# A macaron block of eight batches on one core: first step reordered, last batch's end by tiles, output product in three fp32r passes

## The chip, the core and the metric

The kernel runs on one core of a Trainium2 chip. The core has five engines that work side by side, each through its own list of instructions in order: TensorE (matmuls), VectorE, ScalarE, GpSimd and SyncE, which here issues most of the transfers. They wait for each other through semaphores. TensorE, VectorE, ScalarE and GpSimd read SBUF, TensorE writes PSUM. The metric is the device time of one execution in microseconds; lower is better.

## What is computed

The input x has 8 batches of 512 tokens with 256 channels, all float32. In short:

```
x  = x + 0.5 * adapter(norm(x))             adapter: 8 selected 256x256 matrices, weighted and summed, one bias
h  = layernorm1(norm(x));  hh = h one token earlier
k, v, r = three 256x256 products of (h*tm + hh*(1-tm)), tm its own for each
y  = wkv(k, v): a running, decaying weighted mean over the tokens, made of max and exp
a  = norm(x) + (sigmoid(r) * y) Wo           the output product
h2 = layernorm2(a), shifted and mixed in the same way
kk = relu(h2k Wck)^2  (1024 channels);   kv = kk Wcv;   c = a + sigmoid(h2r Wcr) * kv
x  = x + c
x  = x + 0.5 * adapter(norm(x))
```

## The kernel before

**Stages and steps.** One batch is one unit. Its work is in two halves: the front (first adapter, norm, time mix, k, v, r, wkv, output product, second norm) and the channel part (keys, gate, values, last sum, second adapter). A loop runs over e from 0 to 7. Step e does the channel part of batch e beside the front of batch f = e + 1, and the second adapter of batch e - 1. Ahead of the loop stands the setup, with the adapters' weights and the front of batch 0; behind it the end of the last batch. No planner sets the order: each engine's list is written out by hand, and each semaphore counts up over the whole run.

**TensorE in a step:** `turn_x1(f)` (transposes to channels), keys 0 to 3, `turn_x2(e-1)`, k and v, keys 4 and 5, r, keys 6 and 7, `second_product(e-1)`, the gate product, half of the values of token tile 0, `output_product(f)`, the rest of tile 0 and tile 1, `turn_xa(f)`, tiles 2 and 3. The first adapter, k, v, r, the output product and the values run as float32 (one matmul is two records in the trace). Keys, gate and second adapter run in three fp32r passes instead: each operand is split in a high part (ScalarE's copy to fp32r) and a rest (VectorE's subtraction), and high x high, high x rest and rest x high are summed. The output product is float32: `to_tokens` (L300) with `rwkv` and `wo_sb`, 8 matmuls of 256 columns.

**VectorE in a step:** `value_sum` and `value_stats` of the second half of batch e-1, `mixes(f)` (L848: xr, xk, xv), `gate_input_rest(e)` (L977), `second_rest(e-1)` (L952), `wkv_exponents(f)` (L864: per half a scan over k in PSUM and a subtraction to q), `wkv_states` (L872: a scan and a product per half), denominator, sums, numerator, quotient, `wkv_gated` (L907, ends in `rwkv`, L917), `add_second(e-1)` (L1011), `add_first(f+1)` (L809), `add_output(f)` (L919), `stats_x1`, `norm_output(f)` (L930), the first half of `value_sum(e)`, `norm_first(f+1)`, `mix_ck`, `key_input_rest` (L966), `mix_cr`.

**GpSimd in a step:** the bias for half 1 of batch e-1, a root, `mix_r(f)` (L1161), `hold_exponents(f)` (L1167: clamps of q; L1171 on the second half alone, and `state_exponentials` on ScalarE waits for it), one half of `bias_to_x(f+1)` (L1149) when the sums `aa` are done and the other when `rwkv` is done, `attention_sum(f)` (L1174), roots, and `bias_to_x2(e, 0)` (L1181).

**ScalarE in a step:** `h1_of`, relu and square of the eight key blocks with the high parts and `scaled_difference(f)` (L661, which `mix_r` waits for) between, the exponentials, the reciprocal, the tanh of r and of the gate (`channel_gate`, L626), `residual_of`, statistics of x of batch f+2 from batch `ON_ACT` on (`stats_x`, L530), `h2_of` and what follows it.

**Places.** q, the states and the exponentials share the tile `work`. `xr`, `rwkv`, `xcr` and `xcr_lo` are tiles of 128 x 1024 float32 values. Of the last batch the last sum, transposes and second adapter are done in two halves of two token tiles each.

## Time and profile before

| | us |
|---|---|
| median of 3 runs | 445.81 (445.05 to 447.63) |
| the profiled execution, its whole time | 445.64 |
| its span in the trace | 443.9 |
| busy: TensorE | 426.9 (96%) |
| busy: VectorE | 379.4 (85%) |
| busy: ScalarE | 296.0 (67%) |
| busy: GpSimd | 180.0 (41%) |

The table is from one profiled execution. The span is the time from the first to the last event in the trace; the whole time has a little more around it. An engine is busy while one of its instructions runs. Two records of one engine that follow closely overlap by some 0.08 us, so durations of neighbours sum to slightly more than their distance. Matmul records overlap more: the distance between starts is what one costs. A timeline joins equal instructions in a row: x4 says how many, and the duration is that of all.

### The profile page before, as it was taken

The numbers are of one execution on the slowest core, as the hardware profiler recorded it, in microseconds if no ns is written. First come the engines' busy times: TensorE is split into PE (matmuls) and PEld (weight loads), VectorE is DVE, ScalarE is ACT, GpSimd is POOL, SyncE is SP. The second block draws the span as 40 slices with busy tenths as digits, with TensorE's granted clock in tenths as the row PEclk, the third lists the DMA queues.
The fourth block names the chain that finished last, engine by engine and source line by source line (L and its number), as shares of the span: only waits on it lengthen the run. The fifth ranks groups of instructions, "written<-read, shape, count | busy, mean of one in ns | idle before, by whom it ended". The sixth has DMA issues, their size and how long they took to land. (4 is left out here: it accounts for less than half of the span.)

```text
span 443.9 us, 6124 instructions
## 1 busy us (share of the span) xinstructions
PE 426.9 (96%) x2014; PEld 332.6 (75%) x2014; DVE 379.4 (85%) x769; ACT 296.0 (67%) x541; POOL 180.0 (41%) x161
## 2 busy tenths in 40 slices
PE   8989996989999999999999999999999999999995
PEld 8865873568857885698759885888579865988984
DVE  3989989799999899989999999989998999776134
ACT  1158767695789568984888578956894489736400
POOL 1545053626561465427352746156533444042010
PEclk9999998999999999999999999999999999999999
DMA  6990001001000200011001100010001000100101
GB/s 206 390 396 29 1 0 47 1 1 49 1 0 1 83 13 0 0 50 47 1 0 47 49 1 1 0 48 1 0 1 49 2 0 0 49 0 1 48 1 48
DMA packets 15954, 18.51 MB, mean 42 GB/s; under 512 B 1066, under 2 KB 13618, under 8 KB 15922
## 3 DMA queue, kind: packets, MB, share of 16 engines
q1 hardware_dynamic: 14522, 17.05, 10.8%
q10 hardware_dynamic: 1400, 1.07, 0.8%
q8 instruction: 16, 0.26, 0.2%
q14 instruction: 16, 0.13, 0.1%
HBM read 13.92 MB, written 4.19 MB: 41 GB/s over the span
## 5 line engine op out<-in xcount | busy, mean ns | idle before, releaser
L423 PE MATMUL pair<-wcv_sb,kk 128*128 128x256 f32 x512 | 114.3, 379 | 0.0
L423 PEld LDWEIGHTS pair<-wcv_sb,kk 128*128 128x128 f32 x512 | 96.1, 190 | 12.4
L393 PE MATMUL pair<-xck_hi,wck_hi 128*128 128x512 f32 x128 | 58.0, 453 | 0.7 <-ACT kk L620 0.7
L394 PE MATMUL pair<-xck_hi,wck_lo 128*128 128x512 f32 x128 | 50.6, 395 | 0.0
L397 PE MATMUL pair<-xck_lo,wck_hi 128*128 128x512 f32 x128 | 50.6, 395 | 0.0
L1139 POOL TENSOR_TENSOR x2b<-xs,bias_bc 128x512 f32<-128x512 f32 x15 | 25.6, 1706 | 58.1 <-DVE xs L993 58.1
L1139 POOL TENSOR_TENSOR x<-x,bias_bc 128x512 f32<-128x512 f32 x14 | 18.1, 1298 | 63.4 <-DVE rwkv L917 36.3
L620 ACT ACTIVATE kk<-pair 128x512 f32<-128x512 f32 x64 | 36.4, 594 | 8.1 <-PE pair L397 8.1
L564 ACT ACTIVATE h<-pair,vec 128x512 f32<-128x512 f32 x16 | 11.6, 774 | 42.7 <-PE pair L297 42.7
L624 ACT ACTIVATE kk<-kk 128x512 f32<-128x512 f32 x64 | 37.8, 639 | 0.5
L1119 POOL TENSOR_TENSOR rstd_x<-vare_x,nhalf 128x4 f32<-128x4 f32 (+1 forms) x25 | 30.3, 1213 | 17.5 <-DVE vare_x L777 16.2
L1179 POOL TENSOR_TENSOR xs<-x,xa 128x512 f32<-128x512 f32 x16 | 20.5, 1283 | 39.8 <-DVE xa L923 39.6
L1165 POOL TENSOR_TENSOR xr<-xr,h 128x512 f32<-128x512 f32 x16 | 19.4, 1231 | 35.4 <-ACT xr L666 35.4
L393 PEld LDWEIGHTS pair<-xck_hi,wck_hi 128*128 128x128 f32 x128 | 24.1, 188 | 12.0 <-ACT kk L620 4.1
L325 PE MATMUL pair<-xk,wk_sb 128*128 128x512 f32 x64 | 30.6, 623 | 2.4 <-DVE xk L862 2.4
L394 PEld LDWEIGHTS pair<-xck_hi,wck_lo 128*128 128x128 f32 x128 | 24.1, 188 | 7.7 <-issue 3.3
L306 PE MATMUL pair<-wo_sb,rwkv 128*128 128x256 f32 x128 | 29.0, 380 | 0.4 <-issue 0.4
L325 PE MATMUL pair<-xv,wv_sb 128*128 128x512 f32 x64 | 28.8, 592 | 0.0
L325 PE MATMUL pair<-xr,wr_sb 128*128 128x512 f32 x64 | 28.8, 592 | 0.0
L397 PEld LDWEIGHTS pair<-xck_lo,wck_hi 128*128 128x128 f32 x128 | 24.0, 187 | 6.3 <-DVE xck_lo L971 0.4
L306 PEld LDWEIGHTS pair<-wo_sb,rwkv 128*128 128x128 f32 x128 | 24.2, 190 | 4.0 <-issue 0.7
L875 DVE TENSOR_TENSOR_SCAN work<-work 128x512 f32<-128x512 f32 x16 | 19.6, 1226 | 8.0 <-ACT work L679 8.0
(144 smaller groups left out, 1008.6 us busy)
## 6 DMA issues: line engine op xcount, KB each, us to landing
x<-in_x_dram SPq DMA_DIRECT2D x8, 512.0 KB, 3.5
out_dram<-xs SPq DMA_DIRECT2D x16, 256.0 KB, 2.1
xt<-in_xt_dram SPq DMA_DIRECT2D x4, 512.0 KB, 7.8
work<-in_ffn_w_dram ACTq DMA_DIRECT2D x4, 256.0 KB, 4.5
work<-in_ffn_w_dram SPq DMA_DIRECT2D x4, 256.0 KB, 5.0
kk<-in_wck_dram SPq DMA_DIRECT2D x1, 1024.0 KB, 9.8
xs<-in_xt_dram SPq DMA_DIRECT2D x2, 512.0 KB, 10.9
wcv_sb<-in_wcv_dram SPq DMA_DIRECT2D x1, 1024.0 KB, 12.6
```

What stands on the lines that cost most here:

```text
L306: last = nc.tensor.matmul(bank_of(stage, b, i)[:, t * C:(t + 1) * C], src[:, h, tok:tok + P], w[:, h, :], start=h == 0, stop=h == CH - 1)
L325: last = nc.tensor.matmul(bank, w[:, h, o * P:(o + 1) * P], src[:, h, :], start=h == 0, stop=h == CH - 1)
L393: nc.tensor.matmul(key_bank(n), wck_hi[:, h, cols], xck_hi[:, h, :], start=h == 0, stop=False)
L394: nc.tensor.matmul(key_bank(n), wck_lo[:, h, cols], xck_hi[:, h, :], start=False, stop=False)
L397: last = nc.tensor.matmul(key_bank(n), wck_hi[:, h, cols], xck_lo[:, h, :], start=False, stop=h == CH - 1)
L423: last = nc.tensor.matmul(bank_of("kv", e, i)[:, t % TB * C:(t % TB + 1) * C], kk[:, n, tok:tok + P], wcv_sb[:, n, :], start=n == 0, stop= ...
L620: nc.scalar.activation(kk[:, n, :], key_bank(n), ACT.Relu).then_inc(relu_done, 1)
L624: nc.scalar.activation(kk[:, n, :], kk[:, n, :], ACT.Square).then_inc(sq_done, 1)
L875: nc.vector.tensor_tensor_scan(bb[:, h, 1:PAD], eb_s[:, h, 0:T], eb_v[:, h, 0:T], 0.0, ALU.mult, ALU.add).then_inc(bb_done, 1)
L1119: nc.gpsimd.tensor_tensor(dst, src, power, ALU.pow).then_inc(done, 1)
L1139: nc.gpsimd.tensor_tensor(dst, tile, bias_bc[:, :].rearrange("p (a c) -> p a c", a=1).broadcast_to([P, tiles, C]), ALU.add).then_inc(done, 1)
L1179: nc.gpsimd.tensor_tensor(tok_bank(xs[f % 2], i), tok_bank(x1[f % X1], i), tok_bank(xa, i), ALU.add).then_inc(xs_done, 1)
```

## The change

The output product of batches 1 to 7 is done in three fp32r passes, as the gate product is. Wo gets a high part and a rest once, `rwkv` for each batch: ScalarE copies (`output_input_high`, between the gate's two tanh), VectorE subtracts (`output_input_rest`, between the halves of `add_second`). The high part of `rwkv` lies in the tile of `xr`, its rest in its own tile, and `xcr_lo` now in the tile of `xcr`; `mixes` waits for the output product before it, `past_cr` for the gate product. In every step `gate_input_rest(e)` moves behind `wkv_exponents(f)`, `bias_to_x2(e, 0)` moves into the next step behind the wait for `aa`, and both halves of `bias_to_x` stand behind the wait for `rwkv`. In the first step the statistics of x of batch 2 move from VectorE to ScalarE, the attention sums of batch 0 ahead of the root for `norm_output(0)`, `h1_of(1)` ahead of a square, the high part of the gate's input behind relu 3, and two subtractions of weights behind the mixes and the exponents. The last batch's end goes in three parts: tiles 0 and 1, tile 2, tile 3, each with its own sum, transposes, copy, subtraction, product, addition and store.

```diff
-    ON_ACT = 3
+    ON_ACT = 2
     LAST = B - 1
+    LAST_PARTS = ((0, 1), (2,), (3,))
...
+        def in_place_of(other, name, shape):
+            return nc.alloc_sbuf_tensor_at(name, shape, F32R, offset=place[other])
...
+        wo_hi, wo_lo = sb("wo_hi", [P, CH, C], F32R), in_place_of("wo_sb", "wo_lo", [P, CH, C])
...
-        xcr_lo = sb("xcr_lo", [P, CH, T], F32R)
+        xcr_lo = in_place_of("xcr", "xcr_lo", [P, CH, T])
...
+        rwkv_hi, rwkv_lo = in_place_of("xr", "rwkv_hi", [P, CH, T]), in_place_of("rwkv", "rwkv_lo", [P, CH, T])
...
+            def three_passes(dst, t, own_hi, own_lo, w_hi, w_lo):
+                tok = slice(t * P, (t + 1) * P)
+                passes = [(own_hi[:, h, tok], w[:, h, :]) for h in range(CH) for w in (w_hi, w_lo)]
+                passes += [(own_lo[:, h, tok], w_hi[:, h, :]) for h in range(CH)]
+                for j, (own, other) in enumerate(passes):
+                    last = nc.tensor.matmul(dst, own, other, start=j == 0, stop=j == len(passes) - 1)
+                return last
...
+        LAST_KV = ((3, 0), (3, 1), (0, 0))
+        LAST_Y2 = ((1, 0), (1, 1), (0, 1))
...
+            for j in range(len(LAST_PARTS)):
+                sp.wait_ge(x3_done, 2 * LAST + j + 1)
+                sp.dma_start(some_tiles(tok_dram(out, LAST), j), some_tiles(xs[LAST % 2], j)).then_inc(stored[LAST % 2], 16)
...
             def output_product(f):
                 if f == 0:
                     pe.wait_ge(s_wo, 1)
-                pe.wait_ge(rwkv_done, 2 * f + 2)
-                to_tokens("o", rwkv, wo_sb, xa2_done, f, o_ps)
+                    pe.wait_ge(rwkv_done, 2 * f + 2)
+                    to_tokens("o", rwkv, wo_sb, xa2_done, f, o_ps)
+                    return
+                if f == 1:
+                    pe.wait_ge(s_wo_lo, 1)
+                pe.wait_ge(rwkv_lo_done, 2 * (f - 1) + 2)
+                for i in range(BANKS):
+                    take(pair_of("o", f), i, xa2_done, 2 * f + i + 1)
+                    for t in range(TB):
+                        last = three_passes(bank_of("o", f, i)[:, t * C:(t + 1) * C], i * TB + t, rwkv_hi, rwkv_lo, wo_hi, wo_lo)
+                    last.then_inc(o_ps, 1)
...
-            second_product_part(LAST, 0)
-            turn_x2_part(LAST, 1)
-            second_product_part(LAST, 1)
+            last_values(0, 0, range(HB))
+            last_values(0, 1, range(HB))
+            last_values(1, 2, range(HB // 2))
+            last_turn(0)
+            last_values(1, 2, range(HB // 2, HB))
+            last_values(2, 3, range(HB // 2))
+            last_second(0)
+            last_turn(1)
+            last_values(2, 3, range(HB // 2, HB))
+            last_second(1)
+            last_turn(2)
+            last_second(2)
...
+            def setup_wo_high():
+                nc.scalar.activation(wo_hi[:, :, :], wo_sb[:, :, :], ACT.Copy).then_inc(s_wo_hi, 1)
+            def output_input_high(f):
+                act.wait_ge(r_ps, 2 * f + 2)
+                for h in range(CH):
+                    act.wait_ge(rwkv_done, 2 * f + h + 1)
+                    nc.scalar.activation(rwkv_hi[:, h, :], rwkv[:, h, :], ACT.Copy).then_inc(rwkv_hi_done, 1)
...
             def past_cr(f):
-                past_of("cm_r", f, xcr, (xcr_lo_done, 2 * f))
+                past_of("cm_r", f, xcr, (cr_ps, 2 * f))
...
                 for i in range(BANKS):
+                    if i == BANKS - 1 and has(e + 1):
+                        output_input_high(e + 1)
                     act.wait_ge(cr_ps, 2 * e + i + 1)
                     nc.scalar.activation(tok_bank(thc, i), bank3(bank_of("cr", e, i)), ACT.Tanh, scale=0.5).then_inc(thc_done, 1)
...
             keep_first(5)
+            act.wait_ge(s_wo, 1)
+            setup_wo_high()
+            stats_x(2)
             keep_first(6)
...
                 if has(f) and e > 0:
                     h1_of(f)
                 key_relu(e, 0)
-                gate_input_high(e)
+                if e > 0:
+                    gate_input_high(e)
                 key_square(e, 0)
                 key_relu(e, 1)
-                key_square(e, 1)
                 if e == 0:
                     h1_of(f)
+                key_square(e, 1)
                 key_relu(e, 2)
                 key_square(e, 2)
                 key_relu(e, 3)
                 if e == 0:
+                    gate_input_high(e)
                     keep_first(7)
...
                     if f > 0 and c == 0:
                         dve.wait_ge(r_ps, 2 * f)
+                        dve.wait_ge(o_ps, 2 * f)
                     nc.vector.tensor_tensor(xr[:, c, :], h1[:, c, 1:PAD], h1[:, c, 0:T], ALU.subtract).then_inc(d1_done, 1)
...
+            def output_weight_rest():
+                dve.wait_ge(s_wo_hi, 1)
+                dve.wait_ge(o_ps, CH)
+                nc.vector.tensor_tensor(wo_lo[:, :, :], wo_sb[:, :, :], wo_hi[:, :, :].bitcast(F32), ALU.subtract).then_inc(s_wo_lo, 1)
+            def output_input_rest(f):
+                for h in range(CH):
+                    dve.wait_ge(rwkv_hi_done, 2 * (f - 1) + h + 1)
+                    nc.vector.tensor_tensor(rwkv_lo[:, h, :], rwkv[:, h, :], rwkv_hi[:, h, :].bitcast(F32), ALU.subtract).then_inc(rwkv_lo_done, 1)
...
             def gate_input_rest(f):
                 for h in range(CH):
                     dve.wait_ge(xcr_hi_done, 2 * f + h + 1)
-                    if f > 0 and h == 0:
-                        dve.wait_ge(cr_ps, 2 * f)
                     nc.vector.tensor_tensor(xcr_lo[:, h, :], xcr[:, h, :], xcr_hi[:, h, :].bitcast(F32), ALU.subtract).then_inc(xcr_lo_done, 1)
...
+            def last_sum(j):
+                dve.wait_ge(kv_ps, 2 * LAST + j + 1)
+                dve.wait_ge(thc_done, 2 * LAST + min(j, BANKS - 1) + 1)
+                nc.vector.scalar_tensor_tensor(some_tiles(thc, j), some_tiles(thc, j), 1.0, by_tiles(last_bank(LAST_KV, j), j), ALU.add, ALU.mult).then_inc(kvs_done, 1)
+                dve.wait_ge(kvs_done, 2 * LAST + j + 1)
+                dve.wait_ge(xs_done, BANKS * (LAST + 1))
...
             add_output(0)
+            output_weight_rest()
             norm_output(0)
             stats_x1(1)
             mix_ck(0)
             key_input_rest(0)
             norm_first(1)
             mix_cr(0)
-            second_weight_rest()
-            stats_x(2)
-            gate_weight_rest()
             for e in range(B):
                 f = e + 1
                 if has(e - 1):
@@ -1061,11 +1176,16 @@
                     value_stats(e - 1, 1)
                 if has(f):
                     mixes(f)
+                if has(e - 1) and has(f):
+                    second_rest(e - 1)
+                if e == 0:
+                    second_weight_rest()
+                if has(f):
+                    wkv_exponents(f)
+                if e == 0:
+                    gate_weight_rest()
                 gate_input_rest(e)
                 if has(f):
-                    if has(e - 1):
-                        second_rest(e - 1)
-                    wkv_exponents(f)
                     wkv_states(f)
                     wkv_denominator(f)
                     wkv_sums(f)
@@ -1076,6 +1196,9 @@
                     second_rest(e - 1)
                 if has(e - 1):
                     add_second(e - 1, 0)
+                if has(f):
+                    output_input_rest(f)
+                if has(e - 1):
                     add_second(e - 1, 1)
                 if has(f + 1):
                     add_first(f + 1)
@@ -1085,6 +1208,8 @@
                     stats_x1(f + 1)
                 if has(f):
                     norm_output(f)
+                if e == LAST:
+                    break
                 value_sum(e, 0)
                 value_stats(e, 0)
                 if has(f + 1):
@@ -1093,13 +1218,19 @@
                     mix_ck(f)
...
+            last_sum(0)
+            last_stats(0)
+            last_rest(0)
+            last_sum(1)
+            last_stats(1)
+            last_add(0)
+            last_rest(1)
+            last_sum(2)
+            last_stats(2)
+            last_rest(2)
+            last_add(1)
+            last_bias(2)
+            last_add(2)
...
             pool.wait_ge(s_decay, 2)
             mix_r(0)
             hold_exponents(0)
+            attention_sum(0, 0)
+            attention_sum(0, 1)
             inverse_std("xa", 0)
             first_inverses(1)
-            pool.wait_ge(xck_lo_done, CH)
-            attention_sum(0, 0)
-            attention_sum(0, 1)
             inverse_x(2)
             for e in range(B):
                 f = e + 1
@@ -1209,11 +1338,14 @@
                 if has(f):
                     mix_r(f)
                     hold_exponents(f)
+                if has(e - 1):
+                    if has(f):
+                        pool.wait_ge(aa_done, 2 * f + 2)
+                    bias_to_x2(e - 1, 0)
                 if has(f + 1):
-                    pool.wait_ge(aa_done, 2 * f + 2)
+                    pool.wait_ge(rwkv_done, 2 * f + 2)
                     bias_to_x(f + 1, 0)
-                    pool.wait_ge(rwkv_done, 2 * f + 2)
                     bias_to_x(f + 1, 1)
                 if has(f):
                     attention_sum(f, 0)
@@ -1223,10 +1355,13 @@
                     first_inverses(f + 1)
                 if has(f + 2):
                     inverse_x(f + 2)
-                bias_to_x2(e, 0)
-            for i in range(BANKS):
-                some = slice(i * TB, (i + 1) * TB)
-                pool.wait_ge(vare_done["x2"], LAST + i + 1)
+            for j in range(len(LAST_PARTS)):
+                if j < BANKS:
+                    pool.wait_ge(x2_done, 2 * LAST + j + 1)
+                    pool.wait_ge(x3_done, 2 * (LAST - 1) + 2)
+                    add_bias(some_tiles(x2b, j), some_tiles(xs[LAST % 2], j), len(LAST_PARTS[j]), x2b_parts[j])
+                some = slice(LAST_PARTS[j][0], LAST_PARTS[j][-1] + 1)
+                pool.wait_ge(vare_done["x2"], LAST + j + 1)
                 inverse_root(rstd["x2"][:, some], vare["x2"][:, some], nhalf[:, some], rstd_done["x2"])
```

## Rows read from the trace of the kernel before

**Rows 1.** Busy time by stretch: length, then PE, PEld, DVE, ACT, POOL, granted clock, DMA.

```profile
298.90:346.62 47.72, 47.57 (x226) 36.82 (x226) 44.94 (x91) 32.97 (x55) 22.95 (x20) 1.00 0.04 12
```

**Rows 2.** Chain that ended last (start, us, engine and line).

```profile
347.12 0.88 PE pair L297 x6
...
378.41 2.88 PE pair L319 x24
...
385.85 3.45 PE pair L306 x16
```

**Rows 3.** Timeline of TensorE: the transposes of two steps (start, duration; idle before in brackets).

```profile
346.62 1.38 PE L297 MATMUL pair<-ident,normed 128*128 128x128 f32 x8
...
394.32 1.04 PE L297 MATMUL pair<-ident,normed 128*128 128x128 f32 x8
```

**Rows 4.** Timeline of VectorE and TensorE, one step (start, duration; idle before in brackets).

```profile
316.60 1.21 DVE L867 TENSOR_TENSOR_SCAN work<-decay,pair 128x512 f32<-128x512 f32 x1
...
319.70 0.69 DVE L870 TENSOR_TENSOR work<-work,pair 128x512 f32<-128x512 f32 x1
321.12 1.23 DVE L875 TENSOR_TENSOR_SCAN work<-work 128x512 f32<-128x512 f32 x1 [0.73 <-ACT work L679]
...
323.20 1.23 DVE L875 TENSOR_TENSOR_SCAN work<-work 128x512 f32<-128x512 f32 x1 [0.28 <-ACT work L679]
...
334.53 1.28 DVE L917 TENSOR_TENSOR rwkv<-work 128x512 f32<-128x512 f32 x2
335.73 1.65 DVE L1016 SCALAR_TENSOR_TENSOR xs<-pair,rstd_x,x2b 128x256 f32<-128x256 f32 x4
337.30 1.66 DVE L824 SCALAR_TENSOR_TENSOR x<-xt,rstd_x,x 128x256 f32<-128x256 f32 x4
339.98 0.69 DVE L923 TENSOR_TENSOR xa<-xa,pair 128x512 f32<-128x512 f32 x1 [1.02 <-PE pair L306]
...
341.64 0.69 DVE L923 TENSOR_TENSOR xa<-xa,pair 128x512 f32<-128x512 f32 x1 [0.18 <-PE pair L306]
...
362.36 3.60 PE L325 MATMUL pair<-xk,wk_sb 128*128 128x512 f32 x8
362.92 1.28 DVE L955 TENSOR_TENSOR x2t_lo<-pair,x2t_hi 128x512 fp32r<-128x512 f32 x2
...
364.27 1.22 DVE L867 TENSOR_TENSOR_SCAN work<-decay,pair 128x512 f32<-128x512 f32 x1
```

**Rows 5.** Timeline of GpSimd and ScalarE in the same step.

```profile
320.49 2.01 POOL L1171 TENSOR_SCALAR work<-work,decay 128x512 f32<-128x512 f32 x1 [0.28 <-DVE work L870]
...
335.89 1.29 POOL L1139 TENSOR_TENSOR x<-x,bias_bc 128x512 f32<-128x512 f32 x1 [6.05 <-DVE rwkv L917]
...
335.10 0.60 ACT L631 ACTIVATE thc<-pair 128x512 f32<-128x512 f32 x1 [0.37 <-PE pair L411]
```

**Rows 6.** Timeline where VectorE and GpSimd meet; durations of L1165 (min/median/max).

```profile
76.50 1.29 DVE L982 TENSOR_TENSOR xcr_lo<-xcr,xcr_hi 128x512 fp32r<-128x512 f32 x2
76.82 3.15 POOL L1165 TENSOR_TENSOR xr<-xr,h 128x512 f32<-128x512 f32 x2 [3.27 <-ACT xr L666]
...
L1165 POOL TENSOR_TENSOR xr<-xr,h x16: 1085/1183/2097, 31.8 to 365.2; 128x512 f32<-128x512 f32 x16
...
159.45 2.55 POOL L1139 TENSOR_TENSOR x2b<-xs,bias_bc 128x512 f32<-128x512 f32 x1
...
160.91 2.24 DVE L971 TENSOR_TENSOR xck_lo<-xk,xck_hi 128x512 fp32r<-128x512 f32 x2
```

**Rows 7.** Timeline of the first step.

```profile
75.32 5.36 PE L325 MATMUL pair<-xk,wk_sb 128*128 128x512 f32 x8 [2.39 <-DVE xk L862]
...
79.00 1.22 DVE L867 TENSOR_TENSOR_SCAN work<-decay,pair 128x512 f32<-128x512 f32 x1 [1.21 <-PE pair L325]
```

**Rows 8.** Timeline of VectorE at the end.

```profile
434.59 0.69 DVE L990 SCALAR_TENSOR_TENSOR thc<-thc,pair 128x512 f32<-128x512 f32 x1 [2.14 <-PE pair L423]
...
440.40 0.88 DVE L1016 SCALAR_TENSOR_TENSOR xs<-pair,rstd_x,x2b 128x256 f32<-128x256 f32 x2 [0.59 <-POOL rstd_x L1119]
```

More of the change, by code:

```diff
@@ L32, in build @@
     ROOT = C ** -0.5
-    ON_ACT = 3
+    ON_ACT = 2
     LAST = B - 1
+    LAST_PARTS = ((0, 1), (2,), (3,))
     EARLY = range(2, B)
     with ExitStack() as ctx:
+        place = {}
         def sb(name, shape, dt=F32):
-            return ctx.enter_context(nc.sbuf_tensor(name, shape, dt))
+            tile = ctx.enter_context(nc.sbuf_tensor(name, shape, dt))
+            place[name] = nc.sbuf_base - 4 * math.prod(shape[1:])
+            return tile
+        def in_place_of(other, name, shape):
+            return nc.alloc_sbuf_tensor_at(name, shape, F32R, offset=place[other])
         def sem(name):
@@ L210, in key_bank, with last_bank, some_tiles, some_columns @@
             return pair[key_pair(n)][:, n % 2, :]
+        LAST_KV = ((3, 0), (3, 1), (0, 0))
+        LAST_Y2 = ((1, 0), (1, 1), (0, 1))
+        def last_bank(banks, j):
+            p, i = banks[j]
+            return pair[p][:, i, 0:len(LAST_PARTS[j]) * C]
+        def some_tiles(tile, j):
+            return tile[:, LAST_PARTS[j][0]:LAST_PARTS[j][-1] + 1, :]
+        def some_columns(j):
+            return slice(LAST_PARTS[j][0] * P, (LAST_PARTS[j][-1] + 1) * P)
+        def by_tiles(bank, j):
+            return bank.rearrange("p (t c) -> p t c", t=len(LAST_PARTS[j]))
         def load_adapters(queue, numbers):
@@ L308, in to_tokens, with second_tokens @@
                     last.then_inc(filled, 1)
-            def second_tokens(b, part=range(BANKS)):
-                for i in part:
+            def three_passes(dst, t, own_hi, own_lo, w_hi, w_lo):
[5 more added lines that the diff above has]
+                return last
+            def second_tokens(b):
+                for i in range(BANKS):
                     take(pair_of("y2", b), i, x3_done, 2 * b + i + 1)
                     for t in range(TB):
-                        tok = (i * TB + t) * P
-                        passes = [(x2t_hi[:, h, tok:tok + P], w[:, h, :]) for h in range(CH) for w in (ffn_hi, ffn_lo)]
-                        passes += [(x2t_lo[:, h, tok:tok + P], ffn_hi[:, h, :]) for h in range(CH)]
-                        for j, (own, other) in enumerate(passes):
-                            last = nc.tensor.matmul(bank_of("y2", b, i)[:, t * C:(t + 1) * C], own, other,
-                                                    start=j == 0, stop=j == len(passes) - 1)
+                        last = three_passes(bank_of("y2", b, i)[:, t * C:(t + 1) * C], i * TB + t, x2t_hi, x2t_lo, ffn_hi, ffn_lo)
                     last.then_inc(y2_ps, 1)
@@ L406, in channel_gate @@
                     for t in range(TB):
-                        tok = (i * TB + t) * P
-                        passes = [(xcr_hi[:, h, tok:tok + P], w[:, h, :]) for h in range(CH) for w in (wcr_hi, wcr_lo)]
-                        passes += [(xcr_lo[:, h, tok:tok + P], wcr_hi[:, h, :]) for h in range(CH)]
-                        for j, (own, other) in enumerate(passes):
-                            last = nc.tensor.matmul(bank_of("cr", e, i)[:, t * C:(t + 1) * C], own, other, start=j == 0, stop=j == len(passes) - 1)
+                        last = three_passes(bank_of("cr", e, i)[:, t * C:(t + 1) * C], i * TB + t, xcr_hi, xcr_lo, wcr_hi, wcr_lo)
                     last.then_inc(cr_ps, 1)
@@ L445, in second_product @@
                 second_tokens(e)
-            def second_product_part(e, i):
-                pe.wait_ge(x2t_lo_done, 2 * e + i + 1)
-                second_tokens(e, (i,))
             ffn_setup()
```

114 lines of the change are left out of this document (70 added, 44 removed).

## The prediction

> **What bounds the kernel now.** I read the busy table by step first [rows 1]. A steady step lasts 47.7 us; TensorE is busy for 47.6 of it and VectorE for 44.9. Cutting TensorE work looks like a direct gain. The chain of waits then shows one place in each step where TensorE is not the one that decides: `turn_xa` [rows 2]. Its last six transposes start at 347.12, at the moment at which VectorE ends `norm_output`. The eight take 1.38 us there and 1.04 us in the last step that has them, where VectorE is early [rows 3]: a stall of 0.34 us. So the step is a loop of two engines, and I read VectorE's timeline around it [rows 4]. VectorE starts the first scan of `wkv_exponents` at 316.60, ends `norm_output` at 347.07 (30.47 us), and TensorE needs from there to 364.27 (17.20 us) until the next scan can start. 30.47 + 17.20 = 47.67, the step. The scan at 364.27 follows the end of the subtraction pair of 362.92 (364.20) at once, and the first half of the k product (362.36, 3.60 us for both halves) lands at that time too: VectorE and TensorE arrive together, so nothing saved on VectorE ahead of the scan starts it earlier.
>
> In the 30.47 us VectorE waits four times: 0.73 and 0.28 us for ScalarE between exponents and states, and 1.02 and 0.18 us for the output product in `add_output` [rows 4]. The last two, 1.20 us, are all the slack that its leg of the loop has.
>
> **The change: output product.** Before, 16 records take 3.45 us; the same shape in three fp32r passes is `second_tokens`, 24 records in 2.88 us (378.41) [rows 2]. That is -0.57 us, 7 times, -4.0 us if TensorE decides. It pays with two ScalarE copies of about 0.6 us (as 335.10 [rows 5]) and two VectorE subtractions; a pair of that size takes 1.20 us from its start to the next operation's (334.53 to 335.73) [rows 4]. The pair lies in VectorE's leg: +1.20, against 1.20 of slack. By this alone the product's gain is gone: the leg is as long as before, and TensorE waits longer in `turn_xa`.
>
> **gate_input_rest behind wkv_exponents.** It is 1.20 us taken from before the scan, where nothing is won, and put where VectorE waited 0.73 us. Counted on VectorE alone it costs about 0.1 us. But GpSimd's clamp L1171 starts at 320.49, 0.1 us after the exponents end at 320.39 [rows 5]; it releases ScalarE's exponential and so the second scan of `wkv_states` at 323.20. How such a VectorE pair and a GpSimd operation meet is seen at 76.50: these same subtractions (L982) run undisturbed for 1.29 us, and the GpSimd addition that started at 76.82 takes 2097 ns instead of a median 1183; it ends as if it had started when the pair was done [rows 6]. In the new place the pair would run from 320.33 to 321.6, L1171 from 321.64 to 323.65 instead of 322.50. ScalarE and the second scan follow 1.15 us later (324.35). Nothing behind it waits for anyone until `add_output`, so all of it is in the leg. Bounds: 0.1 (no contention) to 2.3 us (GpSimd gets in between the two halves and the second half waits 2.0 us). I take 1.15, since the row shows this very instruction pair.
>
> **output_input_rest beside bias_to_x.** Before, one GpSimd addition starts when `rwkv` is done (335.89, 1.29 us) and lies beside `add_second`, which reads PSUM and is not disturbed: four in 1.65 us [rows 4, 5]. Now both halves of `bias_to_x` start there and cover 2.6 us, in which VectorE does `add_second(0)` (0.8), the two subtractions, `add_second(1)` and `add_first`. What happens when GpSimd is first: at 160.91 the pair L971, with two SBUF inputs like the new one, takes 2.24 instead of 1.28 us and gets going when the GpSimd addition (159.45 + 2.55 = 162.0) ends [rows 6]. With times from rwkv's end: GpSimd holds 0.1 to 1.4; the first subtraction is ready at 0.8 and ends about 1.95 instead of 1.4: +0.54. If VectorE then keeps its turn, GpSimd's second half runs 2.6 to 3.9 and holds `add_first` up by 0.5; if GpSimd gets in between, the second subtraction loses 1.17. So +1.0 or +1.7; bounds 0 to 1.7; I take 1.0, as at 76.50 GpSimd did not get in between.
>
> The sum for a steady leg is -1.20 + 1.20 + 1.15 + 1.0 = +2.15 us; the step becomes about 49.8 us, and TensorE idles about 3 us in it: `rwkv_lo` is some 1.3 us late for the output product, the rest is at `turn_xa`. This holds for batches 2 to 6, five legs: **+10.8 us**. For batch 7 there is no `bias_to_x` and no `add_first`, and VectorE there waited some 3 us for the product, so 2.4 us more hide: TensorE decides and the step gives -0.6.
>
> The Trainium skill has this contention in the page "SBUF — State Buffer", section "Who interferes with whom": a VectorE instruction with two SBUF inputs and a GpSimd one that reads SBUF exclude each other, and the one that starts first keeps the port for the whole instruction. The trace agrees for subtractions and additions, and differs for scans: that of 321.12 takes its usual 1.23 us while L1171 runs [rows 4, 5]. With the rule applied to scans too, L1171 would be held off one scan more and a leg would cost over 1 us more.
>
> **The first step.** On VectorE `stats_x(2)`, the collision of `norm_first(1)` with GpSimd's sums and two weight subtractions leave the path of k; TensorE's 2.39 us of idling and the half clock behind it (5.36 for what takes 3.60) go too [rows 7]. TensorE's own order then limits: `turn_x1(1)` ends at about 68.0 behind two key blocks, ScalarE's two copies for h take 1.45, VectorE's mixes for k 2.0, so the k product starts about 71.5 instead of 75.32 and the first scan 1.9 us later, 73.4 instead of 79.00: -5.6. It is not kept. `keep_first(7)` and the gate's copies now precede `scaled_difference(1)` on ScalarE, GpSimd's clamps come about 1 us late, and three subtractions in front of L1171 make +1.8 us. From `rwkv` on, subtractions that wait for ScalarE and two additions of GpSimd make +2.9, against a wait of 0.7 us saved. `turn_xa(1)` ends -5.6 + 1.8 + 2.9 - 0.7 = **-1.7 us**. Bounds: -4.3 without contention, 0 if another stall takes it.
>
> **The last batch.** Before, the values end at 434.59 for VectorE, the last addition ends at 440.40 + 0.88 = 441.28 [rows 8]. Now TensorE does the second product of tiles 0 and 1 (half of 2.88) and two transposes (0.22) between the values, which so end 1.7 us later (436.3), but behind them stands one tile instead of two: two sums of about 0.4, transpose and wait 0.5, copy 0.4, subtraction 0.4, six passes 0.7 and 0.3 to land, addition 0.48, with hand-overs about 440.0. With a store of half the size: **-1.5 us**; bounds -2.2 and 0.
>
> **At no cost.** ScalarE's copy of Wo and `stats_x(2)` (about 4.3 us) lie in its wait before `keep_first(6)`; VectorE's subtraction of Wo in its wait for GpSimd before `norm_output(0)` (0.4 us may be lost there, inside the 1.7). `xcr_lo` in xcr and the wait of `mixes` on the output product ask for things done many us before. GpSimd's `bias_to_x2(e,0)` leaves a place where it cost VectorE 0.9 us [rows 6], but ahead of the scan, where it wins under 0.1 us a step. If one of these covers fails it costs its own length once.
>
> **Sum.** -1.7 + 10.8 - 0.6 - 1.5 = +7.0 us on a span of 443.9, so 450.9. The profiled execution took 445.64, 1.74 more than its span, and the median is 445.81: I forecast **452.5 us**.
>
> **Rivals.**
> 1. *No contention (the other side).* GpSimd's clamp and additions slip past the subtractions. A leg then costs +0.1, the first step gives -4.3: -4.3 + 0.5 - 0.6 - 1.5 = -5.9, **440 us**. For: scans and clamps overlap freely. Against: both collisions are in rows with the same kinds of operation. It decides where the contention costs under some 0.9 us a leg (five legs against -2.5, -0.6 and -1.5).
> 2. *TensorE decides throughout.* Then 7 x 0.57, six stalls of 0.34, 4.3 and 1.5 go: **434 us**. It needs VectorE's leg to be 1 us shorter than I find it; rows speak against.
> 3. *One contention only.* L1171 is held off, but the pair behind `rwkv` is not: +1.15 a leg, first step about -3: **446.5 us**, about no change.
> 4. *Worse.* GpSimd gets in between at `rwkv` (+0.7 a leg), or the longer stalls bring the half clock back as at 75.32, at 1.7 us each time: **456 to 461 us**.
> That the product isn't shorter at all I leave out: 24 records of its kind stand at 2.88 us.
>
> **How the numbers follow.** Forecast 0.42, rivals 0.22, 0.08, 0.15 and 0.13. The forecast's own range, from its bounds, is 449.5 to 456; with the rivals down to the first the range is 439 to 456.5. A measurement tells 0.5%, 2.2 us, from no change. Faster: rivals 1 and 2 and a little of 3, 0.33; same: most of 3, 0.10; slower 0.57.
>
> **What would show it.** In the changed kernel: steps of 49 to 50 us from 107 to 346 us; no VectorE wait for ScalarE of 0.7 us between exponents and states, but one over 1 us before the second scan; L1171 at about 3 us instead of 2.01; the first new subtraction at 1.2 us or more; TensorE waiting about 1.3 us before the output product and about 1.5 us at `turn_xa`; the first scan of batch 1 near 73.4. Wrong would be steps under 47.5, or L1171 still at 2.01 us right behind the subtractions.

## The result and the profile after

The changed kernel takes 459.74 us (median of 4 runs, 457.12 to 461.73), the kernel before, run beside it, 445.94 us: ratio 1.0305, 95% interval 1.0277 to 1.0333. Slower, as forecast, but by 13.8 us instead of 6.7, and above the range's upper end of 456.5. The profiled execution took 460.13 us, its span is 458.3.

The table by stretch answers to [rows 1] (start and end of the step, then its length; the number ahead of DMA is the granted clock). The third line is a part of the second step.

```profile
125.52:175.49 49.97, 47.41 (x233) 36.49 (x232) 47.26 (x93) 37.52 (x74) 23.09 (x20) 1.00 0.07 22
175.49:226.51 51.02, 48.74 (x233) 38.04 (x232) 47.45 (x93) 37.51 (x74) 23.11 (x20) 0.97 0.06 21
199.90:203.30 3.40, 3.40 (x18) 3.40 (x17) 3.08 (x8) 2.37 (x11) 0.82 (x1) 0.50 0.23 80
```

The step of 47.7 us is now 49.97 us once and 51.0 us four times (one of these 51.3). The four differ from the one by 3.4 us at half the clock (1.2 GHz instead of 2.4): 18 matmul records fit into 199.90 to 203.30, and the step is 1.05 us longer with it. TensorE's work without it is 47.41 us instead of 47.57; VectorE's is 2.3 us more.

The timeline of VectorE through the second step answers to [rows 4].

```profile
175.49 1.22 DVE L956 TENSOR_TENSOR_SCAN work<-decay,pair 128x512 f32<-128x512 f32 x1 [0.19 <-PE pair L365]
...
179.20 1.28 DVE L1078 TENSOR_TENSOR xcr_lo<-xcr,xcr_hi 128x512 fp32r<-128x512 f32 x2
180.41 1.63 DVE L964 TENSOR_TENSOR_SCAN work<-work 128x512 f32<-128x512 f32 x1
...
182.98 1.23 DVE L964 TENSOR_TENSOR_SCAN work<-work 128x512 f32<-128x512 f32 x1 [0.37 <-ACT work L762]
...
195.51 0.87 DVE L1124 SCALAR_TENSOR_TENSOR xs<-pair,rstd_x,x2b 128x256 f32<-128x256 f32 x2
196.30 2.87 DVE L1069 TENSOR_TENSOR rwkv_lo<-rwkv,rwkv_hi 128x512 fp32r<-128x512 f32 x2
199.09 0.86 DVE L1124 SCALAR_TENSOR_TENSOR xs<-pair,rstd_x,x2b 128x256 f32<-128x256 f32 x2
...
201.71 0.69 DVE L1012 TENSOR_TENSOR xa<-xa,pair 128x512 f32<-128x512 f32 x1 [0.18 <-PE pair L353]
...
207.94 1.38 DVE L1023 TENSOR_SCALAR normed<-xa,mv_xa,rstd_xa 128x256 f32<-128x256 f32 x4
```

The two places of contention are where the prediction put them. `rwkv` ends 20.02 us after the first scan (195.51 - 175.49) instead of 19.13: +0.89, against 1.15 forecast. From there to the addition of the output product are 6.20 us, and 5.94 us in the step without half clock, instead of 4.25: +1.69 even though the wait of 1.02 us is gone; the new pair takes 2.87 us where such a pair takes 1.28 undisturbed (2.79 instead of 1.20 us from its start to the next operation). GpSimd's side of both answers to [rows 5]:

```profile
179.39 2.90 POOL L1302 TENSOR_SCALAR work<-work,decay 128x512 f32<-128x512 f32 x1 [0.28 <-DVE work L959]
...
195.67 2.94 POOL L1270 TENSOR_TENSOR x<-x,bias_bc 128x512 f32<-128x512 f32 x2 [6.05 <-DVE rwkv L1006]
```

The clamp takes 2.90 instead of 2.01 us. The two additions and the two subtractions interleave. One by one they start and last: addition 195.67, 1.27 us; subtraction 196.30, 1.20 us; addition 196.91, 1.71 us; subtraction 197.42, 1.75 us. Undisturbed, an addition takes 1.29 and a subtraction 0.68 us, so the second subtraction is held up by more than the first. This is GpSimd "in between", which the prediction had in its fourth rival.

TensorE's timeline ahead of the output product and of `turn_xa` (first step, then second):

```profile
149.26 0.38 PE L353 MATMUL pair<-wo_hi,rwkv_hi 128*128 128x256 f32 x1 [2.17 <-DVE rwkv_lo L1069]
...
157.79 0.41 PE L334 MATMUL pair<-ident,normed 128*128 128x128 f32 x2 [0.25 <-DVE normed L1023]
...
199.22 0.39 PE L353 MATMUL pair<-wo_hi,rwkv_hi 128*128 128x256 f32 x1 [2.16 <-DVE rwkv_lo L1069]
```

The whole stall stands in one piece ahead of the output product, 2.16 to 2.17 us in five steps, where the forecast had 1.3 there and 1.5 at `turn_xa`. Behind four of the five TensorE falls to half clock 0.7 to 1.0 us after it has resumed.

The first step (VectorE's and TensorE's timelines) answers to [rows 7]; the third line is from the front of batch 7:

```profile
75.50 1.22 DVE L956 TENSOR_TENSOR_SCAN work<-decay,pair 128x512 f32<-128x512 f32 x1 [0.15 <-PE pair L365]
...
92.72 0.36 PE L353 MATMUL pair<-wcr_hi,xcr_hi 128*128 128x256 f32 x1 [3.08 <-ACT kk L702]
...
403.84 0.69 DVE L1012 TENSOR_TENSOR xa<-xa,pair 128x512 f32<-128x512 f32 x1 [1.06 <-PE pair L353]
```

**Where the 14.4 us of span come from.** The first scan of batch 2 starts at 125.52 instead of 125.68: -0.16. The five steps of batches 2 to 6 take 254.37 instead of 238.59 us: +15.78, of it 5 x 2.25 = 11.3 of the longer leg (49.97 against a mean of 47.72), 4 x 1.05 = 4.2 of half clock and 0.3 of the one step of 51.3. From the scan at 379.89 to the end are 78.41 us instead of 79.63: -1.22. In this execution the very first scan also came 1.84 us late (33.87 instead of 32.03), behind a stall of 2.16 us (1.18 before) that ends at 25.67 and a half-clock stretch at 25.8. Other kernels with nearly the same first 30 us had this in some profiles (stalls of 1.90 and 1.83 us there, scans at 33.77 and 33.37) and not in others (stalls of 1.05 us, scans at 32.16 and 32.54).

### The profile page after: what moved, and what is told of

Read it like the earlier page. It is cut to its first block and busy times, and to the rows that moved or that the text cites. A ratio compares the mean times of both kernels' runs of the same rounds, so it can differ in the third digit from the quotient of the medians.

```text
span 458.3 us, 6284 instructions
## 1 busy us (share of the span) xinstructions
PE 430.9 (94%) x2070; PEld 337.9 (74%) x2070; DVE 393.4 (86%) x779; ACT 306.9 (67%) x573; POOL 182.6 (40%) x164
## 3 DMA queue, kind: packets, MB, share of 16 engines
q10 hardware_dynamic: 1400, 1.07, 0.8%
## 5 line engine op out<-in xcount | busy, mean ns | idle before, releaser
L468 PE MATMUL pair<-wcv_sb,kk 128*128 128x256 f32 x448 | 100.5, 380 | 0.0
L468 PEld LDWEIGHTS pair<-wcv_sb,kk 128*128 128x128 f32 x448 | 84.0, 191 | 10.6
L1270 POOL TENSOR_TENSOR x2b<-xs,bias_bc 128x512 f32<-128x512 f32 (+1 forms) x16 | 20.2, 1265 | 97.5 <-DVE xs L1089 48.3
L1270 POOL TENSOR_TENSOR x<-x,bias_bc 128x512 f32<-128x512 f32 x14 | 20.2, 1460 | 42.1 <-DVE rwkv L1006 42.0
L1250 POOL TENSOR_TENSOR rstd_x<-vare_x,nhalf 128x4 f32<-128x4 f32 (+2 forms) x26 | 30.3, 1166 | 8.8 <-DVE vare_x L865 7.3
L353 PE MATMUL pair<-wo_hi,rwkv_hi 128*128 128x256 f32 x56 | 18.6, 346 | 12.1 <-DVE rwkv_lo L1069 11.4
L365 PE MATMUL pair<-xk,wk_sb 128*128 128x512 f32 x64 | 28.9, 594 | 0.6 <-DVE xk L951 0.6
L964 DVE TENSOR_TENSOR_SCAN work<-work 128x512 f32<-128x512 f32 x16 | 22.5, 1403 | 3.6 <-ACT work L762 3.6
L638 ACT ACTIVATE h<-pair,vec,gain 128x512 f32<-128x512 f32 x16 | 11.7, 777 | 20.4 <-PE pair L334 20.3
```

Source lines behind the costliest of these rows:

```text
L353: last = nc.tensor.matmul(dst, own, other, start=j == 0, stop=j == len(passes) - 1)
L365: last = nc.tensor.matmul(bank, w[:, h, o * P:(o + 1) * P], src[:, h, :], start=h == 0, stop=h == CH - 1)
L468: last = nc.tensor.matmul(bank_of("kv", e, i)[:, t % TB * C:(t % TB + 1) * C], kk[:, n, tok:tok + P], wcv_sb[:, n, :], start=n == 0, stop= ...
L964: nc.vector.tensor_tensor_scan(bb[:, h, 1:PAD], eb_s[:, h, 0:T], eb_v[:, h, 0:T], 0.0, ALU.mult, ALU.add).then_inc(bb_done, 1)
L1250: nc.gpsimd.tensor_tensor(dst, src, power, ALU.pow).then_inc(done, 1)
L1270: nc.gpsimd.tensor_tensor(dst, tile, bias_bc[:, :].rearrange("p (a c) -> p a c", a=1).broadcast_to([P, tiles, C]), ALU.add).then_inc(done, 1)
```

## The experiments

Twelve kernels. "Step" is the distance between first scans of `wkv_exponents` in the middle of the run, "stall" TensorE's idle time ahead of the output product there. The expectations, written before each run, call the loop reading "theory V".

**gate_back.** The changed kernel, with the gate's subtractions ahead of the scan again in every step but the first:

```
                 if has(f):
                     mixes(f)
+                if e > 0:
+                    gate_input_rest(e)
                 ...
-                gate_input_rest(e)          (behind wkv_exponents; now only for e == 0)
```

> The changed kernel with gate_input_rest(e) back ahead of second_rest and wkv_exponents for e > 0. Theory V (VectorE's leg from the first scan to norm_output sets the step): the clamp L1302 on GpSimd falls from 2.90 to 2.01 us, the second scan of the states starts 6.6 instead of 7.5 us after the first scan, the step falls from 49.97 to about 49.1 us; TensorE's wait before the output product falls from 2.17 to about 1.25 us and the half clock behind it is gone: about 451 us. Rival T (the late input of the output product and the half clock are the cause, the place of gate_input_rest is not): the clamp shortens but the steps stay at 50 to 51 us: about 459 us.

449.96 us (449.22 to 450.9), ratio 1.0095 (1.0078 to 1.0112). Step 49.06, stall 1.27; the clamp is back at 2.01 us. No half clock in any steady step.

**pool_back.** The changed kernel with GpSimd's additions in their old places: the first half of `bias_to_x` behind `wkv_sums`, `bias_to_x2(e, 0)` at the end of the step.

```
-                if has(e - 1):
-                    if has(f):
-                        pool.wait_ge(aa_done, 2 * f + 2)
-                    bias_to_x2(e - 1, 0)
                 if has(f + 1):
-                    pool.wait_ge(rwkv_done, 2 * f + 2)
+                    pool.wait_ge(aa_done, 2 * f + 2)
                     bias_to_x(f + 1, 0)
+                    pool.wait_ge(rwkv_done, 2 * f + 2)
                     bias_to_x(f + 1, 1)
                 ...
+                if e < LAST:
+                    bias_to_x2(e, 0)
```

> The changed kernel with GpSimd's additions in their old order (one half of bias_to_x after aa, the other after rwkv, bias_to_x2(e,0) at the end of the step). Theory V: one addition instead of two stands beside the subtractions for rwkv_lo; the pair takes about 1.9 instead of 2.87 us, the step falls by about 1.0 to 49.0 us, TensorE's wait before the output product to about 1.2 us, without half clock: about 450.5 us. VectorE loses 0.9 us again at key_input_rest, ahead of the scan, where it costs nothing. Rival (the pair is long because it waits for ScalarE's copies): the pair stays at 2.9 us, about 459 us.

448.98 us (447.75 to 450.04), ratio 1.0071 (1.0045 to 1.0097). Step 48.88, the pair 1.79 instead of 2.87 us, stall 1.07, no half clock in a steady step.

**both_back.** Both edits.

> Both edits together. Theory V: the two savings add in the same leg, steps of about 48.1 us, about 445.5 us, no half clock from batch 2 on. If one of the two hides behind the other, steps stay at 49 and the time at 450.

443.68 us (442.98 to 443.89), ratio 0.9957 (0.9943 to 0.9971). Step 48.07, stall 0.28. Each undo alone gives back some 10 us, both together 16: they overlap in the half clock, which either of them removes by itself. One step of each, by stretch, in the order gate_back, pool_back, both_back:

```profile
174.48:223.54 49.06, 47.41 (x233) 36.57 (x232) 46.87 (x92) 37.45 (x74) 22.20 (x20) 1.00 0.07 22
```

```profile
173.18:222.06 48.88, 47.42 (x233) 36.50 (x232) 46.96 (x92) 37.51 (x74) 23.83 (x20) 1.00 0.07 22
```

```profile
171.03:219.10 48.07, 47.40 (x233) 36.50 (x232) 46.49 (x93) 37.48 (x74) 22.95 (x20) 1.00 0.07 23
```

TensorE's work is the same 47.4 us in all; only its idle time changes.

**fp32_out.** The changed kernel with the output product in float32 again, everything else new.

```
-                last = three_passes(..., rwkv_hi, rwkv_lo, wo_hi, wo_lo)
+                pe.wait_ge(rwkv_done, 2 * f + 2)
+                to_tokens("o", rwkv, wo_sb, xa2_done, f, o_ps)
                 (and without output_input_high, output_input_rest and the split of Wo)
```

> The changed kernel with the output product as float32 as before, without the copies and subtractions for it, the rest unchanged. Theory V: VectorE's leg loses 1.2 us of subtractions and their 1.5 us of contention, but two GpSimd additions now stand beside add_first, which has two SBUF inputs (about +0.95 against the kernel before), and the clamp is still held off (+0.9), so the step is about 48.3 us and not the old 47.7; about 448 us. Rival T (only the product's late input costs): steps of 47.4 us, TensorE decides, about 442 us.

444.86 us (442.41 to 447.98), ratio 0.9987 (0.9962 to 1.0011): no change against the kernel before. Step 48.06. Against the next kernel, which differs by the orders alone, they cost 0.37 us a step and 2.4 us in all: the clamp's delay of about 0.9 us is in good part hidden. VectorE's four longer waits in a step (0.37, 0.44, 1.12 and 0.18 us) are 2.1 us together, and none of them is for the output product. It is with the three passes that the orders cost more.

**start_tail.** The kernel with the new first step and the new end only: float32 product, both orders back.

> The reordered first step and the last batch by tiles alone: gate_input_rest ahead of the exponents, GpSimd's old order and the float32 output product, for every steady step. Theory V: steps of 47.7 us as before, the first scan of batch 2 about 2.8 us earlier than before (122.9 instead of 125.68), the end 1.2 us shorter: about 441.5 us. Rival (in-place tiles and the longer semaphore chains of the changed kernel cost something themselves): steps over 48 us and 444 us or more.

442.50 us (440.39 to 443.62), ratio 0.9925 (0.9899 to 0.9952), step 47.69. It is faster than both kernels, and has the lowest median found; the intervals of both_back and of start_only below touch its own, so that it beats these two is shown by its step alone for both_back and not shown for start_only.

**The dose: pair_twice and pair_thrice.** From both_back, with one or two spare pairs of subtractions (their results go to a tile that nobody reads afterwards) ahead of `output_input_rest`:

```
             def output_input_rest(f):
+                for again in range(1):          (2 in pair_thrice)
+                    for h in range(CH):
+                        dve.wait_ge(rwkv_hi_done, 2 * (f - 1) + h + 1)
+                        nc.vector.tensor_tensor(q[:, h, 0:T], rwkv[:, h, :], rwkv_hi[:, h, :].bitcast(F32), ALU.subtract)
```

In pair_thrice the second spare pair also waits, by a semaphore, for the first.

> From both_back (443.7 us, the three-pass output product with GpSimd's and the scans' old order; step 48.08, TensorE idle 0.28 us before the product, no half clock), with one spare VectorE pair of the same kind (1.2 us) between rwkv and rwkv_lo. The stall theory (the half clock follows a stall of TensorE ahead of the output product): the product starts 1.2 us later, TensorE idles about 1.5 us, step 49.3, so 443.7 + 6 x 1.2 = 451 us; 1.5 lies between the stalls of 1.3 us that had no half clock behind them and those of 1.96 that had one, so half clock in none or all of the steps (457). Slack theory (the product's waits have cover): under 446.

452.35 us (451.94 to 452.56), ratio 1.0146 (1.0118 to 1.0174): step 49.27, stall 1.47, full clock. The slack theory falls, and of the two cases named for half clock it was "in none".

> Two spare pairs (2.4 us). Stall theory: TensorE idles 2.7 us before each output product, 3.4 us of half clock follow in each step, step 48.08 + 2.4 + 1.05 = 51.5, time 443.7 + 6 x 3.4 = 464 us, mean clock about 0.97. Rival, that the half clock comes from the new orders of GpSimd and the scans and not from the stall: step 50.5, clock 0.995, time 458.

464.61 us (463.83 to 467.43), ratio 1.0434 (1.0385 to 1.0483). The stall theory's numbers stand, and the rival's don't: the old orders are in place, and the half clock is back with the stall. From 200.84 on TensorE has 3.4 us of half clock (granted clock 0.51 in 200.80 to 204.20), right behind the stall. The step of pair_twice by stretch, then TensorE's timeline and the step of pair_thrice:

```profile
173.74:223.01 49.27, 47.41 (x233) 36.49 (x232) 47.69 (x96) 37.47 (x74) 22.98 (x20) 1.00 0.07 22
```

```profile
200.41 0.39 PE L354 MATMUL pair<-wo_hi,rwkv_hi 128*128 128x256 f32 x1 [2.65 <-DVE rwkv_lo L1078]
```

```profile
176.23:227.77 51.54, 48.76 (x233) 38.05 (x232) 49.07 (x97) 37.48 (x74) 22.97 (x20) 0.97 0.06 21
```

With these, one sum holds for six kernels with three passes:

| kernel | stall, us | step, us | step - stall, us | half clock in the step |
|---|---|---|---|---|
| both_back | 0.28 | 48.07 | 47.79 | no |
| pool_back | 1.07 | 48.88 | 47.81 | no |
| gate_back | 1.27 | 49.06 | 47.79 | no |
| pair_twice | 1.47 | 49.27 | 47.80 | no |
| changed kernel, 125.52 | 2.17 | 49.97 | 47.80 | no |
| changed kernel, 175.49 | 2.16 | 51.02 | 48.86 | 3.4 us |
| pair_thrice | 2.65 | 51.54 | 48.89 | 3.4 us |

A step is 47.80 us plus the stall, and 1.06 to 1.09 us more where the clock falls. The first spare pair (1.20 us) lengthened the step by 1.20 us: nothing of it is hidden. The sum holds where TensorE has the same work and little other idle time. It doesn't hold for two kernels below, both_stats (stall 0.72, step 49.30) and values_first (0.42, 51.65), where TensorE also idles at other places.

**values_first.** The changed kernel, with all values of tile 0 ahead of the output product, to give TensorE something to do while `rwkv_lo` is late.

```
-                channel_values(e, 0, range(HB // 2))
+                channel_values(e, 0)
                 if has(f):
                     output_product(f)
-                channel_values(e, 0, range(HB // 2, HB))
```

> The changed kernel with TensorE's list edited alone: the whole of token tile 0's values stands ahead of output_product, so 1.73 us more work covers the wait for rwkv_lo. Theory V with the half clock as its second term: VectorE's leg is untouched, so the steps stay at about 49.97 us in all of them, but TensorE's wait before the output product falls from 2.17 to about 0.45 us and the half clock of 3.4 us behind it no longer comes in the steps of batches 3 to 6: 4.2 us less, about 455.5 us. If TensorE's late product were the cause of the long step itself, the steps would fall to 48.3 us and the time to about 447 us; if the half clock has nothing to do with that wait, the time stays at 459 us.

463.34 us (459.26 to 464.87), ratio 1.0363 (1.0277 to 1.0449). A miss of 8 us. TensorE's timeline, and the step and its slow part by stretch:

```profile
199.41 0.39 PE L353 MATMUL pair<-wo_hi,rwkv_hi 128*128 128x256 f32 x1 [0.42 <-DVE rwkv_lo L1068]
...
207.94 1.72 PE L334 MATMUL pair<-ident,normed 128*128 128x128 f32 x8 [1.96 <-DVE normed L1022]
```

```profile
175.68:227.33 51.65, 49.12 (x233) 37.78 (x232) 47.26 (x93) 37.55 (x74) 23.08 (x20) 0.97 0.07 21
208.90:212.30 3.40, 3.40 (x12) 2.87 (x11) 3.33 (x9) 2.72 (x4) 2.56 (x5) 0.51 0.00 0
```

The stall ahead of the product fell from 2.16 to 0.42 us, and the same time appears at `turn_xa`, with the half clock right behind it. The values used there were missing later: TensorE's work is fixed, and VectorE's leg decides when it may go on. Why the step is even 0.6 us longer than in the changed kernel (51.65 against 51.02) no run here separates.

**start_tail_stats and both_stats.** Statistics of `x1` behind `norm_output`, to bring `norm_output` 2 us forward, on start_tail and on both_back.

```
-                if has(f + 1):
-                    stats_x1(f + 1)
                 if has(f):
                     norm_output(f)
+                if has(f + 1):
+                    stats_x1(f + 1)
```

> start_tail with stats_x1(f+1) moved from between add_output(f) and norm_output(f) to behind norm_output(f), VectorE's list alone. Theory V: these 2.0 us leave VectorE's leg, GpSimd's root takes 0.8 of them back as a wait, norm_output ends before TensorE gets to turn_xa, so its stall of 0.34 us per step goes: steps of 47.4 us, about 439.5 us. If the stall is not the bound, 441.5 us as start_tail.

446.76 us (445.48 to 448.39), ratio 1.0028 (1.0002 to 1.0053).

> both_back with the same move of stats_x1. Theory V: VectorE's leg of 48.08 us loses about 1.2 us net (2.0 moved, 0.8 waited for GpSimd's root), TensorE decides again and the shorter output product is worth its 0.57 us: steps of about 46.9 to 47.2 us, about 439 us, at or under start_tail_stats. If the subtractions for rwkv_lo still decide, steps stay near 48 us.

450.47 us (450.11 to 451.13), ratio 1.0104 (1.0039 to 1.0168). Both missed, and in the wrong direction. VectorE's timeline of start_tail_stats:

```profile
249.52 1.38 DVE L1010 TENSOR_SCALAR normed<-xa,mv_xa,rstd_xa 128x256 f32<-128x256 f32 x4 [1.14 <-POOL rstd_xa L1235]
```

The statistics had covered GpSimd's root, which `norm_output` needs. Without them VectorE stands for 1.14 us. `norm_output` does start 0.8 us earlier in both_stats, but the 2.0 us of statistics follow it, so that all behind them comes 1.2 us later, without a pause up to the next scan. VectorE is busy for 46.5 of 48.1 us in both_back (44.9 of 47.7 in start_tail) and can't take that up: 49.30 instead of 48.07, and 48.5 instead of 47.7.

**start_only and tail_only.** The kernel before with the first step's new order alone (on VectorE, ScalarE and GpSimd), and with the end by tiles alone. Of start_only's edit, VectorE's part:

```
-            second_weight_rest()
-            stats_x(2)
-            gate_weight_rest()
             for e in range(B):
                 ...
+                if e == 0:
+                    second_weight_rest()
                 if has(f):
                     wkv_exponents(f)
+                if e == 0:
+                    gate_weight_rest()
+                    gate_input_rest(e)
```

> The kernel before with the first step's new order alone (second_weight_rest, the statistics of batch 2 and gate_weight_rest out of VectorE's way ahead of the first scan of batch 1). If the gain of start_tail (442.5 against 445.4) is the sum of its halves: 445.4 - 1.5 = 443.9, with the scan of batch 2 some 1.5 to 2.8 us earlier; if all of it is the end's, 445.4.

443.47 us (442.58 to 444.61), ratio 0.9940 (0.9919 to 0.9962).

> The kernel before with the last batch's end by tiles alone. From the last scan of exponents to the end 78.2 us against 79.6: 445.4 - 1.4 = 444.0; if the end by tiles gains nothing by itself, 445.4.

444.31 us (444.08 to 446.44), ratio 0.9969 (0.9947 to 0.9990). Each gains by itself, 2.4 and 1.6 us; together in start_tail 2.9 (against 445.44 of the kernel before, run beside it); start_tail's runs spread over 3.2 us, so whether the two add up is not settled. In tail_only the last scan of exponents starts at 364.30 and the span is 442.5: 78.2 us instead of 79.6.

## Why the prediction was wrong

**Right: what bounds the step, and the sign.** The loop of two engines stands: VectorE's leg from scan to `norm_output` grew and the step with it. In the step without half clock the leg is 158.21 - 125.52 = 32.69 us (`norm_output` starts at 156.92; and the next operation follows 1.29 us later, as 207.94 to 209.23), +2.22 against a forecast of +2.15, and TensorE's part is 17.28 against 17.20. A step of "about 49.8" was 49.97. The rival without contention (440 us) falls with the clamp at 2.90 us and the pair at 2.87.

**Right in sum, wrong in the parts.** The part up to `rwkv` cost 0.9 instead of 1.15. From there to `add_output` it was +1.69, where the forecast's terms give 1.20 + 1.0 - 1.02 = +1.18: GpSimd's second addition did get in between, the case that I valued at +0.7 and put into the fourth rival, because it had not happened at 76.50 [rows 6]; `add_first`, which I had held up by 0.5, was not (1.58 us from 149.92 to 151.50). These 0.5 us came back: some 0.25 by the smaller first term, 0.1 at `add_output`'s second wait (152.88 - 151.50 = 1.38 us between its two additions instead of 1.66, of which 0.18 was in the forecast) and 0.1 behind it. That the sum came out within 0.1 us is luck.

**The step that failed: the fourth rival.** The prediction had TensorE idle 3 us in every step, split the idle time in two (1.3 and 1.5 us), and counted the half clock at nothing, with "the longer stalls bring the half clock back" in a rival at 0.13. The stall is one piece of 2.17 us, because all of VectorE's delay lies ahead of `rwkv_lo` and what is behind it did not grow; four of five such stalls were followed by 3.4 us at half clock, at 1.05 us each: 4.2 us. The measured 459.7 us lies in that rival's 456 to 461, which had half of its mechanism and a price of 1.7 us where 1.05 was paid. The row that should have warned is [rows 7]: 2.39 us of idling in a TensorE that is otherwise busy, and 5.36 us for what takes 3.60. A chain that brings TensorE 2 to 3 us of stall in each step should have had this in its likeliest case. pair_thrice shows that a longer stall is enough to bring it, with the old orders and the same product. It is no certainty: tail_only has the idle time of [rows 7] too (2.38 us, up to 75.27), and its product takes 3.70 us, at full clock.

**The balance.** Forecast +7.0 on the span, measured +14.4. The difference of 7.4: 4.2 half clock, 0.5 the leg (5 x 0.10), 0.3 the one longer step, 1.5 the first step and 0.9 the last stretch.

**First step.** Counted from the very first scan, the first scan of batch 1 came 5.34 us earlier (41.63 instead of 46.97; forecast 5.6), and batch 2's 2.00 us earlier (91.65 instead of 93.65; forecast 1.7). So the term was about right; the profiled execution lost 1.84 us ahead of it to the stall and the half clock at 25.8, whose cause no run here settles. start_only agrees: -2.4 us in its time, and 1.55 us from the first scan to that of batch 2 (92.10 instead of 93.65).

**Last batch.** -1.5 forecast, -1.43 in tail_only's span and -1.6 in its time. That the stretch from 379.89 gained only 1.22 in the changed kernel lies in the step of batch 7, put at -0.6: from its first scan to its `turn_xa` it takes 30.27 us (410.16 - 379.89) instead of 30.05, so +0.2. There too TensorE waits for `rwkv_lo` (0.58 us, up to 402.04), and VectorE only 1.06 us for the product instead of 2.78. From `turn_xa` to the end are 48.14 instead of 49.58 us, -1.44.

**The product.** From its start to the next operation's it takes 2.95 us (192.80 to 195.75 in both_back) instead of the 3.45 of [rows 2]: -0.50, against -0.57. TensorE's busy time fell by 0.2 us a step only (47.60 to 47.41 between start_tail and both_back); the step grew by 0.38. What the passes cost depends on what else is in the leg: 0.38 us a step in the old orders, 3.0 us (51.03 against 48.06) in the new ones, while the new orders cost 0.37 with the float32 product. Neither edit is expensive; together they overrun the slack.

**Open.** Five kernels (gate_back, pool_back, both_back, pair_twice, both_stats) have one step that is 0.7 to 1.0 us longer than its neighbours (49.00 in both_back beside 48.07, 49.80 in gate_back), where one small VectorE operation on 128x4 values takes 0.60 to 1.20 us instead of 0.17; nothing in the profile explains it. In others it is 0.3 to 0.5 us, or there is none. Why the clock stayed full behind the stall at 149.26 is open as well: that of 2.17 us was followed by none, one of 1.96 us (values_first) was. In the first step the stall of 3.08 us ahead of the gate product had half clock begin behind it in the changed kernel (92.72) and in pair_thrice, and none at all near it in gate_back, both_back, start_tail and values_first. So longer stalls brought half clock in most steps here, and what decides whether and when it comes these runs don't show.

## What to carry to other kernels

Where two engines close a loop and both are over 94% busy, add up the slack of the leg once and charge every edit against the same sum: two edits that are nearly free alone (0.4 us a step each) cost 3.3 together. Where a TensorE stall of about 2 us appears in an otherwise full step, put a half-clock stretch behind it into the forecast itself, and look first for the edit whose removal shortens the stall: stalls of 1.47 us and less cost their own length and no more here. Filling the stall by moving TensorE's work only moved it here, and independent work in front of an operation may be the cover of another engine's result: look who is late when it is gone.

## What the runs showed that I had not expected

- **A scan is not free of GpSimd.** The scan of `wkv_states` took 1.225 to 1.227 us in all 16 cases before. In the changed kernel it takes 1.63 us where the clamp was queued behind a pair of subtractions and both became ready together (180.41), and 1.23 us where the clamp already ran. The prediction had called scans undisturbed, and set beside it the rule of the Trainium skill ("SBUF — State Buffer", section "Who interferes with whom"), by which a scan would hold the clamp off for its whole length. That would have cost over 1 us a leg; the delay is 0.41 us, on the scan's side. So neither was right: as I read it, the scan loses where it becomes ready together with a clamp that was held up, and not where it finds the clamp running. What passes between the two engines then, the trace doesn't show.
- **Half clock comes in stretches of 3.4 us** (6.8 us in five profiles, at about 90 us or at 311 in values_first). In steps from batch 2 on it came at 15 of 16 stalls of 1.93 to 2.68 us, between 0.6 us before TensorE resumed and 1.4 us after; it never came at those of 1.07 to 1.47 us. Its price in the step was 1.05 us of the 1.7 that 3.4 us at half speed lose; where the other 0.65 us hide was not tried.
- **Who starts first decides whether GpSimd gets between the halves of a pair.** Where GpSimd's addition was already running (195.67), additions and subtractions took turns, and the pair took 2.87 us; with a single addition beside it (pool_back) it is 1.79 us. Where the pair had just started (179.20, and 76.50 in [rows 6]), it took its 1.28 us, and GpSimd's operation was held up behind both halves.
